# Opening of an adaLN attention kernel: first weight scales spread by TensorE, first head's weight parts made on three engines

## What is computed

```python
mod = (_silu(L0_c) @ L0_wmod).reshape(L0_c.shape[0], 6, 1, -1)
sa, ca, ga, sb, cb, gb = (mod[:, 0], mod[:, 1], mod[:, 2], mod[:, 3], mod[:, 4], mod[:, 5])
h = _layernorm(x, axis=-1) * (1 + ca) + sa
# attention on h, per matrix m in q, k, v, o:
w = codes * jnp.repeat(scales, block_size, axis=0)      # block_size 32
q = x @ w + bq                                          # k and v alike
scores = jnp.einsum('bqhd,bkhd->bhqk', q, k) / jnp.sqrt(jnp.float32(HEAD_DIM))
attn = jax.nn.softmax(scores, axis=-1)
out = jnp.einsum('bhqk,bkhd->bqhd', attn, v).reshape(B, S, NUM_HEADS * HEAD_DIM)
x = x + ga * (out @ w_o + bo)
# then the second layer norm and the routed layer, x + gb * ffn(h)
```

## Time and profile before

| | us |
|---|---|
| median of 3 runs | 777.8 |
| lowest, highest | 777.14, 778.07 |
| the profiled execution, its own time | 777.42 |
| its span in the trace | 775.5 |
| TensorE busy | 766.5 (99% of the span) |
| VectorE busy | 647.5 (83%) |
| ScalarE busy | 517.6 (67%) |
| GpSimd busy | 483.4 (62%) |

### The profile page before, as it was taken

How to read it: one execution, slowest core, us unless ns; L and a number is a source line. 1 busy time by engine, 2 the same in 40 slices (tenths; PEclk the granted TensorE clock), 3 DMA queues, 4 the chain that set the end, 5 groups by cost and what they waited for, 6 DMA issues and landing times.

```text
span 775.5 us, 14722 instructions
## 1 busy us (share of the span) xinstructions
PE 766.5 (99%) x4206; PEld 667.7 (86%) x4206; DVE 647.5 (83%) x1254; ACT 517.6 (67%) x1124; POOL 483.4 (62%) x454
## 2 busy tenths in 40 slices
PE   7999999999999999999999999999999999999998
PEld 6888888888888888888888888888888888888887
DVE  5889888888888888888888888888898888879876
ACT  2788676667666676667666766676667676766841
POOL 4686576548655675556657575655667476789722
PEclk9999999999999999999999999999999999999999
DMA  7554355444454335444445434543355334433202
GB/s 216 162 154 124 95 147 150 139 107 99 118 144 131 95 96 139 129 124 98 110 133 147 98 94 122 146 125 95 96 145 152 95 94 107 112 89 86 56 1 109
DMA packets 71898, 90.67 MB, mean 117 GB/s; under 512 B 19574, under 2 KB 37431, under 8 KB 71867
## 3 DMA queue, kind: packets, MB, share of 16 engines
q1 hardware_dynamic: 53184, 74.00, 37.3%
q10 hardware_dynamic: 18682, 16.30, 7.0%
HBM read 22.06 MB, written 2.11 MB: 31 GB/s over the span
## 4 chain that ended last, share of the span: by engine, by line
PE 95%; POOL 1%; DVE 1%; DMA 1%; ACT 1%; SPq 1%; issue 0%; DVEq 0%
PE score L1102 9%; PE score L1103 9%; PE score L1104 9%; PE qv L1102 8%; PE qv L1103 8%; PE qv L1104 8%; PE o L1102 7%; PE o L1104 7%; PE o L1103 7%; PE ky L1102 4%; PE ky L1103 4%; PE ky L1104 4%; PE y L1102 2%; PE y L1104 2%; PE y L1103 2%; DMA stage<-in_L_attn_wk_scales_dram 1%
## 5 line engine op out<-in xcount | busy, mean ns | idle before, releaser
L404 POOL TENSOR_TENSOR pT_lo<-pT,pT_hi 128x512 fp32r<-128x512 f32 x248 | 314.6, 1305 | 240.7 <-ACT pT_hi L576 240.6
L660 ACT ACTIVATE prob<-score,neg_max 128x512 f32<-128x512 f32 x256 | 172.7, 688 | 79.7 <-DVE neg_max L941 79.5
L941 DVE TENSOR_REDUCE neg_max<-score 128x1 f32<-128x512 f32 x256 | 159.7, 682 | 1.6 <-PE score L1104 1.6
L954 DVE STREAM_TRANSPOSE pB<-prob 128x512 f32<-128x512 f32 x252 | 156.4, 678 | 0.0
L576 ACT ACTIVATE pT_hi<-pT 128x512 fp32r<-128x512 f32 x248 | 135.3, 620 | 0.0
L1102 PE MATMUL score<-k_hi,q_hi 128*128 128x512 f32 x256 | 101.2, 395 | 0.6 <-DVE k_lo L862 0.6
L1103 PE MATMUL score<-k_lo,q_hi 128*128 128x512 f32 x256 | 100.3, 392 | 0.0
L1104 PE MATMUL score<-k_hi,q_lo 128*128 128x512 f32 x256 | 99.7, 389 | 0.0
L1102 PE MATMUL o<-pT_hi,v_hi 128*128 128x512 f32 x248 | 96.6, 389 | 0.0
L1104 PE MATMUL o<-pT_hi,v_lo 128*128 128x512 f32 x248 | 96.5, 389 | 0.0
L1103 PE MATMUL o<-pT_lo,v_hi 128*128 128x512 f32 x248 | 96.5, 389 | 0.0
(11 more groups left out here) (262 smaller groups left out, 1824.7 us busy)
## 6 DMA issues: line engine op xcount, KB each, us to landing
pT<-pB SPq DMA_DIRECT2D x1008, 64.0 KB, 2.0
out_dram<-x_nat SPq DMA_DIRECT2D x8, 256.0 KB, 2.1
stage<-in_L_attn_wv_codes_dram ACTq DMA_DIRECT2D x7, 256.0 KB
stage<-in_L_attn_wv_scales_dram ACTq DMA_DIRECT2D x14, 128.0 KB
stage<-in_L_attn_wq_codes_dram ACTq DMA_DIRECT2D x7, 256.0 KB
stage<-in_L_attn_wq_scales_dram ACTq DMA_DIRECT2D x14, 128.0 KB
stage<-in_L_attn_wk_codes_dram ACTq DMA_DIRECT2D x7, 256.0 KB
stage<-in_L_attn_wk_scales_dram ACTq DMA_DIRECT2D x14, 128.0 KB
```

Source lines behind the costliest of these rows:

```text
L404: pool.tensor_tensor(split(pT_lo, kt), turned(par, kt), split(pT_hi, kt).bitcast(f32), ALU.subtract).then_inc(p_lo_ok, 1)
L660: act.activation(prob[:, i], score_ps[i][:, :], ACT.Exp, bias=neg_max[:, i:i + 1], accum_out=row_sum[:, s % 2, i:i + 1]).then_inc(exp_ok, 1)
L941: dve.tensor_reduce(neg_max[:, i:i + 1], score_ps[i][:, :], AX.X, ALU.max, negate=True).then_inc(max_ok, 1)
L954: dve.transpose(pB[:, s % 2, :, i].rearrange("p g k q -> p k g q"), prob[:, i].rearrange("p (k g q) -> p k g q", k=QT, g=G)).then_inc(pB_o ...
```

## The change

The first scales of q, k and v are no longer read 32 times. ScalarE's queue loads each as four rows of one partition each (`load_rows`) into buffers of 128 partitions that VectorE has set to zero; a 128x128 matrix `block_rows` with ones where row a meets its block of 32 columns is made on VectorE; TensorE multiplies them (`spread_rows`, two f32 matmuls of 128x256 for each matrix) into a PSUM bank, and VectorE makes the product codes times scales from there (`first_product`), for q and k in two halves by head. The first-pair products of k and v thus leave GpSimd. Of head 0's parts, q stays on GpSimd, k's rounded part is made by ScalarE and its rest by VectorE. `hT_hi` of c = 1 goes to ScalarE, the bias vectors too. The normalisation of batch 1 goes from ScalarE to VectorE and stands behind the first four maxima; its statistics stand around `k_lo`. The fill transposes are cut from 20, 14 and 10 to 6, 4 and 8. The transpose of the bias vectors stands ahead of that of the first batch. On SP, 12 DMAs of scales are gone.

```diff
+        block_rows = pB[:, 0, 1, 0]
+        scale_rows = dict(q=gb_row[:, 0:2], k=gb_row[:, 2:4],
+                          v=pB[:, 0, 0].rearrange("p i k q -> p (i k q)").rearrange("p (c n) -> p c n", c=2))
...
             queue.dma_start(codes[m][:, :, :], rows).then_inc(ld_w_first[m], 16)
-            for a in range(NB):
-                src = bass.AP(SCALES[m].tensor, a * row, [[0, BLK], [half, 2], [1, PW]])
-                queue.dma_start(scales[m][at[a]:at[a] + BLK], src).then_inc(ld_w_first[m], 16)
+            if m == "o":
...
+        def load_rows(queue, m):
+
+            src = bass.AP(SCALES[m].tensor, 0, [[FEAT, NB], [NB * FEAT, 2], [1, PW]])
+            queue.wait_ge(rows_zero, 1 + "qkv".index(m))
+            queue.dma_start(scale_rows[m][0:NB], src).then_inc(ld_rows[m], 16)
...
             inverse_std(0)
             parts("q", 0, 0)
-            product("k", 0)
-            parts("k", 0, 0)
+            parts("v", 0, 0)
+            inverse_std(1)
             parts("q", 0, 1)
-            inverse_std(1)
-            product("v", 0)
-            parts("v", 0, 0)
             parts("k", 0, 1)
...
         def _(act):
+            load_rows(act, "q")
+            load_rows(act, "k")
+            act.wait_ge(c_tr, 1)
+            act.activation(c_exp[:, :], qv_ps[:, 0:B * DC], ACT.Exp, scale=-1.0).then_inc(c_exped, 1)
+
+            load_rows(act, "v")
...
+            act.wait_ge(vec_tr, 1)
+            act.activation(vecT[:, NH:VECS], score_ps[1][:, NH:VECS], ACT.Copy).then_inc(vec_ok, 1)
+            act.activation(vecT[:, 0:NH], score_ps[1][:, 0:NH], ACT.Copy, scale=SCORE_SCALE).then_inc(vec_ok, 1)
...
+            act.wait_ge(h_ev, 2)
+            act.activation(hT_hi[:, 1, tokens(0)], hT32[:, 1], ACT.Copy).then_inc(h0_hi, 1)
+            act.wait_ge(w_half["k"], 1)
+            act.activation(w_hi["k"][head_cut(0)], w32["k"][head_cut(0)], ACT.Copy).then_inc(w_hi_ok["k"], 1)
...
             k_high(1, 0)
-            normalise(1, range(QT))
...
+            for m in "qkv":
+                dve.memset(scale_rows[m], 0.0).then_inc(rows_zero, 1)
+            dve.memset(block_rows, 0.0).then_inc(block_zero, 1)
...
+            dve.tensor_copy(block_rows[0:NB], ident[0:NB, 0:NB].unsqueeze(2).to_broadcast([NB, NB, BLK])).then_inc(block_ok, 1)
...
+            first_product("q", 0)
+            first_product("k", 0)
+            input_hi(0, 0)
+            input_lo(0, 0)
+            input_lo(0, 1)
+            dve.wait_ge(w_hi_ok["k"], 1)
+            dve.tensor_tensor(w_lo["k"][head_cut(0)], w32["k"][head_cut(0)], w_hi["k"][head_cut(0)].bitcast(f32),
+                              ALU.subtract).then_inc(w_ok["k"], 1)
+            first_product("v", 0)
             dve.wait_ge(vec_ok, 2)
-            dve.wait_ge(ld_x[1], 16)
-            statistics(1)
...
                     maximum(3)
+                    if start:
+                        normalise(1)
...
-            for i in range(20):
+            for i in range(6):
                 pe.transpose(score_ps[0][:, (i % QT) * P:(i % QT + 1) * P], ident[:, :], ident[:, :])
+
+            def spread_rows(m):
+                pe.wait_ge(block_ok, 1)
+                pe.wait_ge(ld_rows[m], 16)
+                for c in range(2):
+                    ins = pe.matmul(first_scales(m)[:, c], block_rows[:, :, :].rearrange("a b q -> a (b q)"), scale_rows[m][:, c],
+                                    start=True, stop=True)
+                ins.then_inc(rows_mm[m], 1)
```

More of the change, by code:

```diff
@@ L771, in _ @@
             dve.wait_ge(silu_step, 2)
-            dve.tensor_tensor(c_silu[:, :], c_exp[:, :], o_ps[0][:, 0:B * DC], ALU.mult).then_inc(silu_ok, 1)
+            dve.tensor_tensor(c_silu[:, :], c_exp[:, :], qv_ps[:, 0:B * DC], ALU.mult).then_inc(silu_ok, 1)
             steps = [0]
@@ L841, in _, with first_product @@
             normalise(0)
[L842 to L850, removed]
+            def first_product(m, j):
+                dve.wait_ge(ld_w_first[m], 16)
+                dve.wait_ge(rows_mm[m], 1)
+                cut = head_cut(j) if m in "qk" else (slice(None), slice(None), slice(None))
+                dve.scalar_tensor_tensor(out=w32[m][cut], in0=codes[m][cut], scalar=SCORE_SCALE if m == "q" else 1.0,
+                                         in1=first_scales(m)[cut], op0=ALU.mult,
+                                         op1=ALU.mult).then_inc(w_half[m] if m in "qk" and j == 0 else w_prod[m], 1)
+            first_product("q", 0)
[7 more added lines that the diff above has]
+            first_product("v", 0)
             dve.wait_ge(vec_ok, 2)
-            dve.wait_ge(ld_x[1], 16)
-            statistics(1)
             def q_low(count, head):
@@ L902, in _ @@
             q_low(1, slice(0, 1))
+            dve.wait_ge(ld_x[1], 16)
+            row_statistics(1, 0)
+            row_statistics(1, 1)
             k_low(1, slice(0, 1))
+            row_statistics(1, 2)
+            row_statistics(1, 3)
+            variances(1)
+            first_product("q", 1)
+            first_product("k", 1)
             def head_slice(p, s):
@@ L984, in pair @@
                             magnitude_guard(2 * (s - 4))
-                        q_low(n + 2, head_slice(p, s + 1))
+                        if not start:
+                            q_low(n + 2, head_slice(p, s + 1))
                         if start:
@@ L1130, in transpose_input @@
                     ins.then_inc(h_tr, 1)
+            pe.wait_ge(ld_vec, 16 * 3)
+            pe.transpose(score_ps[1][:, 0:VECS], vec_raw[:, :], ident[0:VECS, 0:VECS]).then_inc(vec_tr, 1)
             transpose_input(0)
-            pe.wait_ge(ld_vec, 16 * 3)
-            pe.transpose(o_ps[1][:, 0:VECS], vec_raw[:, :], ident[0:VECS, 0:VECS]).then_inc(vec_tr, 1)
-            for i in range(14):
-                pe.transpose(score_ps[0][:, (i % QT) * P:(i % QT + 1) * P], ident[:, :], ident[:, :])
+            spread_rows("v")
+            for i in range(4):
+                pe.transpose(qv_ps[:, (i % QT) * P:(i % QT + 1) * P], ident[:, :], ident[:, :])
             def project(dst, m, j, b, by_half=False):
@@ L1162, in _ @@
             project(ky_ps, "k", 0, 0).then_inc(k_mm, 1)
-            for i in range(10):
-                pe.transpose(score_ps[0][:, (i % QT) * P:(i % QT + 1) * P], ident[:, :], ident[:, :])
+            pe.wait_ge(vec_ok, 2)
+            for i in range(8):
+                pe.transpose(score_ps[1][:, (i % QT) * P:(i % QT + 1) * P], ident[:, :], ident[:, :])
             def weighted(n, vpar, j):
```

58 lines of the change are left out of this document (38 added, 20 removed).

## The result

The changed kernel takes **781.17 us** (median; 780.18 to 782.37) against 777.78 (777.14 to 778.41) for the kernel before: ratio 1.0045, interval 1.0034 to 1.0055. It is slower by 3.4 us, where 2.0 was forecast, and lies 0.2 us above the top of the range. Its profiled run took 780.87 us, span 779.0 (before 777.42 and 775.5).

What follows compares the result with a forecast made beforehand. TensorE was taken as full from 60 to 740 us, so the opening's shift carries one for one to the end. Terms -2.8 + 1.6 + 1.7 + 1.5 = +2.0 gave 779.8 us, range 776.4 to 781.0.

Steps and rivals of the forecast that it cites:

- case A: The forecast as summed: turns on the memory path and a halved clock behind the long wait, 779.8 us; chance 0.42.
- up to the first scores: Opening, before the first sweep: first score matmul at 17.65 instead of 20.43 us, 2.8 us gained.
- longer list on VectorE: First sweep, k_lo end to v_lo end: VectorE's list takes 7.9 us instead of 6.3, 1.6 us lost.
- turns with GpSimd: Batch 1's normalisation on VectorE alternates with GpSimd on SBUF: 1.7 us lost, bounds 0.6 and 3.3.
- half clock behind the wait: TensorE idles 4.1 us before the first sweep's k projection, then runs at half clock: 1.5 us lost, between 0 and 1.7.
- Modulation at 7.00: Opening: the modulation matmuls on TensorE start at 7.00 us, with the rows landed by 5.4.
- Case E: Opening: rows or vectors land late and TensorE waits, each us late a us lost, 778.8; chance 0.18 together with Case C.
- Spread matmuls: Opening, TensorE: 0.24 us each, 0.48 at half clock; four ahead of the modulation fit in time that fills held before.
- The transposes and what follows them: Opening: transposes start at 9.4, hT32 for c = 0 at 10.16, hT_lo for c = 0 by 12.2 us.
- The spread of v: Opening, TensorE: v's two matmuls, 0.5 to 1.0 us, and 4 fills replace 14 fills; q projection starts at 12.2.
- nothing behind that gives it back: After the second sweep's first scores, the 2.0 us delay stays to the end.
- Case C: Opening: modulation at half clock, 3.3 us not 2.12; 778.1 to 779.2 without the late fall; chance 0.18 together with Case E.

Runs made afterwards that it cites:

- experiment 3: Changed kernel plus 28 fill transposes on TensorE between the first sweep's q projection and its wait for v_lo: 778.9 us, ratio 1.0017.
- experiment 2: Changed kernel with GpSimd held, from k's parts of the second head on, until batch 1's four normalisations are through: 778.62 us, ratio 1.0013.
- experiments 5: Changed kernel with GpSimd held until batch 1's normalisation ended, 12 fills before the v_lo wait, SP's large loads held until wmod landed: 777.98 us, ratio 1.0009.
- 7: Changed kernel with batch 1 on all three engines as in the kernel before, and SP's large loads held until wmod landed: 777.15 us, ratio 0.9988.
- 6: Changed kernel with batch 1's normalisation back on ScalarE behind q_hi and SP's large loads held until wmod landed: 778.13 us, ratio 1.0002.
- 9: Kernel of experiment 7 plus three fill transposes on TensorE ahead of the wait for c: 776.29 us, ratio 0.998.
- Experiment 1: Changed kernel with batch 1's normalisation back on ScalarE, behind q_hi of the first sweep: 778.73 us, ratio 1.0005.
- experiments 4: Changed kernel with SP issuing k's codes and all later loads only once wmod has landed: 780.39 us, ratio 1.0027.
- 8: Changed kernel without the three row loads of the scales, so its scales are not those of the weights: 782.05 us in the one run.
- 10: Changed kernel plus only three fill transposes on TensorE ahead of the wait for c: 781.42 us, ratio 1.0048.

## Why the prediction missed, step by step

The direction and each mechanism of case A stood; the sizes add up as follows (us of the profiled runs, from the landmarks).

| step | forecast | measured | from |
|---|---|---|---|
| up to the first scores | -2.8 | -1.35 | 20.43 to 19.08; -2.4 to +0.25 in experiments 3 and 2 |
| longer list on VectorE | +1.6 | +1.3 | 7.71 (exp. 2) less 6.39 |
| turns with GpSimd | +1.7 | +1.5 | 9.22 less 7.71 (exp. 2) |
| half clock behind the wait | +1.5 | +1.3 | 5.08 less 3.78; exp. 3 |
| second sweep | 0 | +0.7 | 12.05 less 11.31 |
| sum | +2.0 | +3.5 | 780.87 less 777.42 |

**First failed step: the gain of the opening, 2.8.** In the changed kernel's run it was 1.35, and in none of the five profiles with this opening, or nearly this one, 2.8. Four things that the prediction laid beside other work, or had too short, were on the path, in a row:

- *wmod and the vectors.* "Modulation at 7.00" was taken as fixed. It started at 8.02, 0.44 of it waiting for wmod, whose landing had moved from 4.9 to 5.9 us. Case E named rows and vectors, not wmod. The vectors were 0.35 late (0 to 0.5 forecast).
- *Spread matmuls.* They were priced at 0.24 each from the sixteen of the earlier trace rows; but a record count is not a call count: the four matmuls of q and k stand as eight records, and took 3.6 us at half clock, up to 7.6. So they alone put the modulation at 7.6, and the wait for wmod adds 0.44. In experiments 5 and 7, without a wait for wmod, it starts at 7.38 and 7.20.
- *The transposes and what follows them.* They began at 10.52, behind the late modulation and the vectors, and took 1.88, not 1.09: the clock fell at 10.66, close to the 10.8 of the kernel before, but the work then stood a microsecond further back. So `hT` for c = 0 was begun at 11.64 and not 10.16, and `hT_lo` for c = 0, which the first q matmul waits for, was ready at 13.60:

```profile
12.91 0.69 DVE L854 TENSOR_TENSOR hT_lo<-hT,hT_hi 128x512 fp32r<-128x512 f32 x1
```

- *The spread of v* took 1.7 us (12.18 to 13.89), not 0.5 to 1.0, and with four fills behind it put the q projection at 14.34 and not 12.2. Only some 0.7 us of that was on the path, as the q projection had to wait for the 13.60 anyway; in experiments 3 and 5, at full clock there, TensorE did wait for `hT_lo`, 0.47 and 0.53 us.

Part of it was given back: the projections then ran at full clock, so that the last q matmul was 1.3 late and not 2.1. At the first scores it was 1.4.

**Second failed step: "nothing behind that gives it back", and nothing takes more.** The prediction looked for turns only at the normalisation. The same turns hit the second cast of `hT_hi` in the second sweep: +0.7. The forecast slowdown, 2.0 us, was thus too small by 1.4 us for the opening and 0.7 for the second sweep, while the three losses between them came out 0.7 smaller than forecast.

**Right:** the premise that a shift is carried one for one; the 1.5 us for `wk_lo` gone, `k_hi` without a wait for it; the length of the way to `v_lo` (9.2 against 9.6); the turns, chosen between bounds of 0.6 and 3.3 from the single row; the clock, down from 27.7 to 31.1 against "28 to 31". That an instruction waits as long as the other engine's runs agrees with the Trainium skill (page "SBUF — State Buffer", section "SBUF: two separate sides"); who comes next, which it leaves open, the rows show: they alternate.

**Case C was real too,** though not in the changed kernel's profile: in experiments 2, 6 and 9, and partly in 1, the modulation ran at half clock. Three more fills ahead of `c` didn't decide which of the two a run takes. The profiles show one difference. In 2, 6 and 9, and in no other, TensorE stood idle ahead of k's spread matmuls, waiting for k's scale rows, and there the modulation took 3.41 or 3.42 us:

```profile
6.60 2.05 PE L1175 MATMUL y<-gb_row,pB 128*128 128x256 f32 x4 [0.62 <-DMA gb_row<-in_L_attn_wk_scales_dram]
```

The row is that of experiment 2; the gaps in 6 and 9 are 0.28 and 0.42 us. These are the rows that case E was afraid of; the prediction had them landed by 5.4. Experiment 1 is different: its clock was up by 6.1 us (four records of the spread in 1.03 us) and fell at 9.5, behind the wait of 1.58 for wmod, for 6.8 us. No experiment changes only the arrival of k's rows, so that this gap is the cause isn't shown. **Open** are this and the part of wmod's delay that the large loads don't explain. The kernel before, with 20 fills up to 7.00, spreads less in the last comparison (777.0 to 778.0) but reached 779.6 in the first; more fills ahead of the modulation were not tried in the changed kernel.

## What to carry to other kernels

Work that leaves a late engine must not go to the engine that the next wait ends on: ask of the receiving engine's list whom TensorE waits for behind it, and what that engine's instructions meet on SBUF. Dropping loads brings the others forward, and an early critical load may pay for it: look at when it lands, and try its wait ahead of the large ones. Keep the good half: the spread scales and shared parts of head 0, with batch 1 as it was, came out 0.1 to 0.2% faster than the kernel before; the whole change is 0.45% slower.

## What the runs showed of the hardware

- VectorE instructions with two SBUF inputs alternate with GpSimd's, one by one, as long as GpSimd has one waiting: four normalisations take 3.16 us in place of 1.66. The cast of `hT`, with one SBUF input, waits too: 1.41 in place of 0.43. GpSimd's `hT_lo` becomes ready only when the first cast has ended: a second cast right behind the first is ahead of it (0.78 and 0.84 for both), one that comes 0.19 to 0.43 us later finds GpSimd at work.
- An f32 matmul of 256 columns stands as two records, together some 0.9 us at half clock (1.71 for two).
- Behind the wait of 3.4 us the clock fell from 1.00 to 0.50 in every kernel that left it empty (after, experiments 4, 8 and 10), for 3.4 us or, in 8, for 6.8; in experiment 2 it fell behind 1.89 us, in 1 and 6, with 0.8, it did not. With transposes in the stretch it held (28 in experiment 3; 12 behind a wait of 1.54 in 5).
- A stretch before the first clock record shows a PEclk of 1.00 though matmuls run at half clock; there the duration of one matmul tells it (16 of the modulation: 1.95 or 3.42 us).
